# A new order for the SyncE queue and for GpSimd in the delta rule of a two-layer model

## The reference

```python
def step(S, inp):                       # per value head; S is 128 x 128
    qt, kt, vt, gt, bt = inp
    S = S * jnp.exp(gt)[:, None, None]
    kv = jnp.einsum('hk,hkv->hv', kt, S)
    delta = (vt - kv) * bt[:, None]
    S = S + kt[:, :, None] * delta[:, None, :]
    o = jnp.einsum('hk,hkv->hv', qt, S)
    return (S, o)
...
q = jnp.repeat(_l2norm(q), KV_RATIO, axis=2) * DK ** (-0.5)
k = jnp.repeat(_l2norm(k), KV_RATIO, axis=2)
...
gated = core * jax.nn.silu(z)
gated = gated * jax.lax.rsqrt(jnp.mean(gated * gated, axis=-1, keepdims=True) + EPS)
return (gated * norm_w).reshape(B, Tn, VDIM) @ W_out
```

## Time and profile before

| | |
|---|---|
| time of 3 runs, median | 2949.89 us (2949.39 to 2954.56) |
| profiled execution | time 2948.88 us, span 2945.6 us |
| TensorE busy | 2667.0 us, 91% of the span |
| VectorE, ScalarE, GpSimd busy | 2208.7, 1793.3, 1510.1 us |
| mean granted clock of TensorE | 0.971 |

### The profile page before, as it was taken

The page is one execution under the profiler, slowest core; times in us unless marked ns, Lnnn a source line. Parts: engine busy times, 40 slices in busy tenths (PEclk is TensorE's granted clock), DMA queues, the critical chain, the costliest instruction groups (busy, mean ns, idle before and its releaser), DMA issues. The chain is left out here.

```text
span 2945.6 us, 78514 instructions
## 1 busy us (share of the span) xinstructions
PE 2667.0 (91%) x25327; PEld 1828.5 (62%) x25327; DVE 2208.7 (75%) x4805; ACT 1793.3 (61%) x6310; POOL 1510.1 (51%) x3737
## 2 busy tenths in 40 slices
PE   5999579999999999999999999999999999769998
PEld 4556256666666666666666666666666666655555
DVE  3433468888888888888888888878887888637776
ACT  3322557777777776777767776767676777332332
POOL 1000456666666666676666666767666667310000
PEclk9999889999999999999999999999999999879999
DMA  3000132222222222222222222222222222110000
GB/s 90 0 1 0 29 62 44 56 44 52 45 51 50 55 48 48 51 44 56 41 60 44 56 44 52 44 51 46 56 51 48 48 47 47 26 44 1 8 8 15
DMA packets 522444, 122.31 MB, mean 42 GB/s; under 512 B 460160, under 2 KB 521200, under 8 KB 522032
## 3 DMA queue, kind: packets, MB, share of 16 engines
q1 hardware_dynamic: 522032, 117.16, 19.3%
HBM read 89.01 MB, written 28.06 MB: 40 GB/s over the span
## 5 line engine op out<-in xcount | busy, mean ns | idle before, releaser
L557 POOL TENSOR_TENSOR Tb<-Tb,btmp 64x14 f32<-64x14 f32 (+6 forms) x896 | 317.5, 354 | 72.2 <-issue 1.8
L553 POOL TENSOR_TENSOR btmp<-Bk,Tb 64x14 f32<-64x14 f32 (+6 forms) x896 | 315.4, 352 | 60.4
L1156 DVE SCALAR_TENSOR_TENSOR R<-bank,gs,xn 128x128 f32<-128x128 f32 x512 | 156.0, 346 | 236.9 <-PE bank L622 236.6
L1064 ACT ACTIVATE gatn<-gat,ty 128x128 f32<-128x128 f32 x512 | 163.5, 390 | 251.2 <-POOL ty L531 251.2
L1271 DVE SCALAR_TENSOR_TENSOR S<-S,gs,bank 128x128 f32<-128x128 f32 x1024 | 286.1, 340 | 29.4 <-PE bank L815 29.4
L542 POOL TENSOR_TENSOR Tb<-Bk,lower 64x256 f32<-64x256 f32 x64 | 55.9, 874 | 481.8 <-DMA Bk<-blk_n 448.3
L1302 DVE SCALAR_TENSOR_TENSOR conv<-raw,ckq,conv 128x512 f32<-128x512 f32 x384 | 286.1, 759 | 14.0 <-ACT conv L1045 4.9
L1302 DVE SCALAR_TENSOR_TENSOR conv<-raw,cv,conv 128x512 f32<-128x512 f32 x384 | 282.6, 750 | 9.1
L962 ACT ACTIVATE oq<-bank,gs 128x128 f32<-128x128 f32 x512 | 162.9, 378 | 183.6 <-PE bank L633 183.6
L787 PE MATMUL bank<-wz_h,xnT 128*128 128x256 f32 x1024 | 255.3, 394 | 0.0
L771 PE MATMUL bank<-xnT,wkq 128*128 128x512 f32 x512 | 242.4, 617 | 10.6 <-POOL mkX L438 10.6
(11 more groups left out here) (365 smaller groups left out, 7092.4 us busy)
## 6 DMA issues: line engine op xcount, KB each, us to landing
Wp<-blk_w SPq DMA_DIRECT2D x384, 64.0 KB
rowb<-decay_rows SPq DMA_DIRECT2D x256, 64.0 KB, 3.9
blk_n<-N SPq DMA_DIRECT2D x256, 64.0 KB, 2.2
Tp<-blk_t SPq DMA_DIRECT2D x128, 128.0 KB, 2.8
wkq<-in_L_attn_W_qkvz_dram SPq DMA_DIRECT2D x32, 128.0 KB, 2.2
wv<-in_L_attn_W_qkvz_dram SPq DMA_DIRECT2D x16, 256.0 KB, 2.6
Bk<-blk_n SPq DMA_DIRECT2D x64, 64.0 KB, 2.5
blk_t<-Tb SPq DMA_DIRECT2D x64, 64.0 KB, 2.5
```

The source lines that it names most:

```text
L553: pool.tensor_tensor(tmp, Bk[:, j, j + 1:].unsqueeze(2).broadcast_to([64, 15 - j, j]), Tb[:, j, 0:j].unsqueeze(1).broadcast_to([64, 15 - j ...
L557: pool.tensor_tensor(Tb[:, j + 1:, 0:j], Tb[:, j + 1:, 0:j], tmp, ALU.subtract).then_inc(row_rdy, 1)
L1064: i = act.activation(gatn[:, u, :], gat[:, u, :], ACT.Copy, scale=ty[t.c][:, SC, u:u + 1])
```

## The change

On SP, `decays` works on step n - 1 in slot n and no longer on step n: a step's decay rows are now loaded in the slot in which `clamp` reads them. `base_out` is cut in two: `base_send` (Tb and Wb to DRAM) and `base_receive` (Tp and Wp from DRAM). `dump` is moved from behind the weights to between the two. On GpSimd, `derive`, `scaled` and `causal` are moved ahead of `base_rest` and `base_first`, and the fourteen rows are divided anew: rows 1 and 2 in `base_first`, 3 to 11 in `base_middle`, 12 to 14 in `base_rest`. No instruction of the steady slots is added or removed on any engine, and TensorE, VectorE and ScalarE keep their order.

```diff
                 def decays(s):
 
-                    t = s.back(S_F - 2)
+                    t = s.back(S_F - 1)
...
-                def base_out(s):
+                def base_send(s):
...
                     sp.dma_start(blocks(wd), Wb[:]).then_inc(w_out, 16)
+
+                def base_receive(s):
+
+                    t = s.back(S_F + 3)
+                    if not t.live or t.c % 2:
+                        return
+                    sent, solved = (held(sp, v) for v in (t.pairs(16, 16), t.at(1, -2)))
+                    r = t.c // 2 % 2
                     sp.wait_ge(m["made"], 2)
                     wait(sp, t_out, sent)
                     wait(sp, x16_mm, solved)
...
                 def body(s):
                     decays(s)
-                    base_out(s)
+                    base_send(s)
+                    dump(s)
+                    base_receive(s)
                     value_weights(s)
                     key_weights(s)
                     gate_weights(s)
                     out_weights(s)
-                    dump(s)
                     base_load(s)
...
                 def base_first(s):
...
-                    for j in range(1, 4):
+                    for j in range(1, 3):
...
                 def base_middle(s):
...
-                    for j in range(4, 11):
+                    for j in range(3, 12):
...
                 def base_rest(s):
...
-                    for j in range(11, ROWS + 1):
+                    for j in range(12, ROWS + 1):
...
                 def body(s):
                     step_gates(s)
                     halo(s)
-                    base_rest(s)
-                    base_first(s)
                     derive(s)
                     scaled(s)
                     causal(s)
+                    base_rest(s)
+                    base_first(s)
                     out_scale(s)
                     base_middle(s)
                     norm_scale(s)
```

More of the change, by code:

```diff
@@ L358, in base_out @@
                         return
-                    rows, made, before, w_before, sent, solved = (held(sp, v) for v in (
-                        t.pairs(ROWS, ROWS), t.pairs(1, 1), t.pairs(32), t.pairs(96), t.pairs(16, 16), t.at(1, -2)))
-                    r = t.c // 2 % 2
+                    rows, made, before, w_before = (held(sp, v) for v in (
+                        t.pairs(ROWS, ROWS), t.pairs(1, 1), t.pairs(32), t.pairs(96)))
                     sp.wait_ge(m["made"], 2)
```

## The result

| | before | after |
|---|---|---|
| median | 2952.22 us (2949.39 to 2955.58, 4 runs) | 3075.3 us (3072.89 to 3086.31, 4 runs) |
| profiled span | 2945.6 us | 3067.9 us |
| mean granted clock | 0.971 | 0.956 |

The changed kernel is slower: 1.0424 times the time before, 95% interval 1.0395 to 1.0452. The forecast was +27 us; measured were +123. The direction and the loop of SP and ScalarE came as forecast. The size did not, and the time lies outside the range.

A forecast was written before the change was run, and what follows sets the result against it. Pairs were bound by SP's queue, the late clamp and gatn, plus GpSimd's 0.7 us. Per eight slots: key weights +1.0, the pair behind -0.2, two typical +0.5 each, +1.8; fifteen times, +27: 2976 us, range 2905 to 3036.

The forecast's parts named there:

- the loop of SP and ScalarE: SP's queue to the decay rows, then ScalarE from clamp to gatn, sets each pair of slots: 33.4 to 33.5 us.
- What bounds the kernel: A slot lasts until gatn is made, plus 1.33 us to its transposes, plus 4.48 to the next slot.
- GpSimd's gain: Start slots, with `out_scale` no longer behind Bk: up to 1.1 us a pair, up to 4.5 behind key weights.
- Step 1: SP's send slot: `dump` waits for N until 9.4 us, and the eight loads of Tp and Wp queue behind it.
- GpSimd's 0.7: GpSimd's 16.0 us chain to Wb's copy delays `dump` from 9.4 to 10.1 of the send slot: pair 34.15 us.
- The 0.8 more that two stretched row operations would have cost: GpSimd's row chain: two operations stretched by 0.4 us each through contention with VectorE would add 0.8 a pair.
- Step 2: SP's queue: `dump` 1.35 us, eight loads 5.37 plus 0.4 for stretching; Bk issued at 16.5, decay rows at 17.4.
- Step 3: Landing of the decay rows: both transfers there 4.2 us after the first issue, at 21.6 from the send slot's begin.
- the rival in which they slow each other: Loads, Bk and decay rows issued without a pause land later: each pair costs 1 us more, 3036 us; chance 15%.
- Step 4: ScalarE in the start slot: clamp 2 to 3 us late; from clamp to gatn 6.0 us without the old waits.
- Step 5: The pair: 21.6 + 6.0 + 1.33 + 4.48 = 33.4 to 33.5 us, against 33.66 before.
- Covered at nothing: Other delayed SP loads, Wp, Tp, Bk and a send slot's decay rows, were taken to land in time, at no cost.

The follow-up runs named there:

- decays_early: The changed kernel with `decays` back at its old lag, loading one step ahead, nothing else undone: 2907.18 us, 0.9858 of the kernel before.
- dump_back: The changed kernel with `dump` back behind the weights, send and receive together: 3200.2 us, 1.0858 of the kernel before.
- gate_first: The changed kernel with the gate's weights issued at the head of the slot, ahead of `dump`'s wait: 3072.18 us, 1.0406 of the kernel before.
- weights_first: decays_early with all weights issued right behind the decay rows, ahead of everything that waits for GpSimd or VectorE: 2876.77 us, 0.9749 of the kernel before.

## Why the prediction was right in direction and wrong in size

**What bounds the kernel.** Right for the kernel before, and close in time for the changed one, but there by other links: in start slots TensorE waits for R and oq, not for gatn. In ordinary pairs without the gate's weights the transposes follow gatn's begin by 1.7 us on average (1.33 forecast) and the next slot them by 4.75 (4.48). In the pair of 1206.38 gatn is made by 1237.20, and TensorE comes to the transposes at 1238.18, from L823 and L757 at the low clock.

**GpSimd's gain.** Right in kind, by decays_early: start slots of 15.8 where no weights are loaded. Behind key weights 1.8 of the "up to 4.5" came (20.2 to 18.4).

**Step 1 and GpSimd's 0.7, the place of `dump`.** Right: 10.25 of the send slot in ordinary pairs, 10.1 forecast. The 16.0 us chain of GpSimd was well summed (16.2 in ordinary pairs). That `dump` itself is a gain was not seen; dump_back shows it. The 0.8 more that two stretched row operations would have cost did not come: row 3 took 0.24 in the pair shown (1235.23).

**Step 2, the burst of issues.** 0.3 short: from Tp's first issue to Bk's took 6.1 on average in pairs without key weights, 5.77 forecast. The row of Tp x2 shows it, 1.89 against 1.27.

**Step 3, the landing: the step that failed first.** I read "3.3/3.7/4.2" as both transfers landed 4.2 after the first issue. The numbers are each from its own issue, and the 4.2 belongs to the second, which is issued 0.8 later: the data are there 5.0 after the first. The trace of before shows it for all 128 pairs of these loads: the second takes longer than the first, 4.1 against 3.3 at the median. Now the first issue to the clamp takes 4.8 on average (3.9 to 5.9) in pairs without key weights. For the two transfers at 1225.30 the trace gives

```profile
DMA to landing us min/median/max: 3.2/3.6/4.0
```

and 4.0 + 0.8 is the 4.80 of the timeline. The transfers are no slower than before, median 3.9 us in both kernels. So the rival in which they slow each other did not happen; that its time of 3036 was the nearest is chance. The step costs 0.6 us a pair. With 0.3 of step 2 and small ones the clamp of an ordinary pair without the gate's weights runs 23.6 us after the send slot's begin, not 22.3.

**Step 4, from clamp to gatn.** Right: 5.82 on average, 6.0 forecast.

**Step 5, the pair: the clock, a second step that failed.** I priced a lower clock for pairs with key weights alone. But in every start slot TensorE is now idle for 1.4 us or more, 2.4 on average without key weights, and in some the clock falls too. The start slot of 1223.89, cut into stretches (the third number from the end is the granted clock):

```profile
1230.00:1236.00 6.00, 4.37 (x67) 2.72 (x65) 3.51 (x8) 5.90 (x22) 2.17 (x7) 1.00 0.06 13
1236.00:1240.00 4.00, 3.81 (x19) 3.49 (x20) 2.55 (x7) 1.93 (x7) 3.29 (x10) 0.57 0.20 46
1240.00:1243.37 3.37, 3.37 (x19) 2.68 (x18) 2.93 (x4) 2.94 (x14) 2.98 (x6) 1.00 0.02 5
```

After the gap the clock is 0.57 for four us: mostly the lower of its two levels, 1.2 of 2.4 GHz. That falls on the transposes and the gate's projection, on the path. This slot is not typical. Of the 46 start slots without key weights 13 show a granted clock of 0.84 to 0.92 and the other 33 show 1.00. In the 13 gatn to the next slot takes 7.7 us on average, in the 20 at full clock that load no gate weights 5.85, as forecast (5.81). Spread over the ordinary pairs that load none it makes the 0.65 us by which these two steps are longer than forecast (0.38 + 0.27). Behind key weights the clock falls in all 14, and TensorE's busy time is 18.4 there, 2.4 more than at full clock, where I had put 1.6. In all steady slots it is 37.7 us net of what the kernel before lost already. The size of one fall was in the page before: 17.65 against 16.02. How many slots would have one it did not tell.

**Covered at nothing: a term missed.** My list had Wp, Tp and Bk, and not the weights, though they too stand behind `dump` now. SP in the start slot of 1986.12, and TensorE:

```profile
1996.75 1.27 SPq L402 DMA_DIRECT2D blk_n<-N  x2
1998.24 0.42 SPq L315 DMA_DIRECT2D wz_h<-in_L_attn_W_qkvz_dram  x1
```

```profile
2001.36 1.99 PE L795 MATMUL bank<-wz_h,xnT 128*128 128x256 f32 x8 [0.95 <-DMA wz_h<-in_L_attn_W_qkvz_dram]
```

wz_h waits until `dump` has its N, 10.6 into the slot, and lands a us too late. It is the order of SP's body with an instruction that waits moved ahead of ones that don't. In the changed kernel it costs 17.4 us of waits, which gate_first shows to be swallowed by the other loop; in weights_first, where there is no other loop, its removal counts.

**Key weights and the pair behind.** 39.3 against 38.5 forecast, and 35.1 against 33.5: the pair behind is not the bare loop of 33.5, its path has the same 1.6 of landing, bursts and clock as the others.

**The sum.** For eight slots I had 1.8 us more; it is 7.7. Of the missing 5.9, 0.8 are in the pair with key weights, 1.6 in the one behind it, and 1.7 in each ordinary one; the rest is rounding, and that 14 and not 15 pairs have key weights. Fifteen times 5.9 are 88 us, and the filling adds 7, which I had left as it was. The sign was thin, 0.5 us a pair, less than the error of step 3 alone, so it came right with some luck: nearly all errors pointed the same way. With steps 3 and 5 at their measured size (0.6 in each of 60 pairs, 0.65 in each of 45), the forecast would have been 65 us higher, 3041, still 34 short.

**What would show it.** L542's idle time down from 481.8 us to 53, ScalarE idle at the clamp by 3 to 4 us (2 to 3 said) and 6.5 behind key weights (5 and more said), `dump` at 9.4 to 10.8 (9.4 to 10.1 said) and the decay rows at 18.5 in ordinary pairs (17 to 18 said): all but the sizes came.

Between decays_early and the changed kernel lies one slot of lead for loads that take 3.9 us at the median from issue to landing, and 168 us of time. A rule of the Trainium skill bears on it (DMA: Bandwidth & Descriptors, Rules for kernel authors): issue a DMA early and wait for it late, so that its fixed cost lies beside other work. The traces agree with it: with the slot of lead the clamp's 286.4 us of waits are gone.

## What to carry to other kernels

A load's lead in a software pipeline is part of its price: before moving a load to the slot that reads it, sum the queue ahead of it from its last waiting instruction on, each issue with its duration, and the landing of the last transfer from its own issue. In a queue that is worked in order, what waits for another engine belongs behind what waits for nothing; whenever a waiting instruction is moved forward, every load behind it needs a look, weights too. Where two loops share one resource, a relief of the one shows in the next slot of the other: time it in the whole kernel before it is counted as a gain, and price gaps on TensorE's path with the clock's loss that rows of the same kernel show, with a range for how often it comes.

## What was not expected of the hardware

The clock's loss comes in two sizes, and whether it comes can't be told from the idle time. Of the changed kernel's 60 start slots 27 show it: a granted clock of 0.91 or 0.92 over the slot with TensorE busy for 17.5 to 18.0 us (the last steady slot apart, at 14.0), or one of 0.84 to 0.86 with 18.6 to 19.1, against 16.0 to 16.3 at full clock. All 14 behind key weights are among them. The one of 2022.63, in stretches:

```profile
2032.00:2034.00 2.00, 0.20 (x16) 0.06 (x4) 0.00 (x0) 1.91 (x5) 0.00 (x0) 1.00 0.00 0
2034.00:2036.00 2.00, 0.02 (x2) 0.05 (x2) 1.86 (x4) 2.00 (x12) 0.41 (x3) 0.76 0.00 0
2036.00:2038.00 2.00, 2.00 (x30) 2.00 (x32) 1.26 (x4) 2.00 (x7) 1.76 (x5) 0.50 0.15 32
2038.00:2040.00 2.00, 2.00 (x23) 1.66 (x18) 0.96 (x4) 1.20 (x5) 1.53 (x7) 0.50 0.65 161
2040.00:2042.00 2.00, 2.00 (x10) 1.88 (x9) 1.97 (x5) 0.53 (x1) 1.76 (x4) 0.53 0.55 155
2042.00:2045.53 3.53, 3.53 (x20) 2.84 (x18) 3.10 (x5) 3.10 (x15) 3.14 (x6) 1.00 0.10 31
```

TensorE does 0.22 us of work in four, the clock falls within them, and the six us after the gap run at half of it; then it is whole again. The slot's TensorE work takes 18.78 us instead of 16.0. So in this slot 4.1 us without work cost nearly 7 (22.9 against 16.0), and 1.8 us in the slot of 1223.89 cost 3.5. But there is this start slot too, in the same run:

```profile
1040.93:1060.46 19.53, 16.03 (x181) 11.38 (x180) 14.57 (x32) 12.31 (x46) 12.35 (x31) 1.00 0.20 39
```

It is idle for 3.5 us, in three gaps, and keeps the full clock. The slot of 1223.89 is idle for 1.8, in two gaps, and falls to 0.91. Both take 19.5 us. No run here shows what decides it. Over the span the same 25327 matmuls were busy 2667.0 us before, 2708.8 in the changed kernel, and 2647.9 with the early decay rows: a third of what the steady slots grew by is this, and it is seen by comparing TensorE's busy time for an unchanged instruction count, which no list of waits shows.

Open stay: when the clock falls and when it doesn't, and whether dividing the rows 3, 8, 3 gains anything over 2, 9, 3. The new place of `dump` by itself (with the old lag and GpSimd's old order) was not run either.
